# Two moves of small vector sums at the seams of a two-layer decoder: behind the router's last weights, and behind the first norm of the latent layer

## The reference, cut to what matters

```python
x = x + linear_attention(norm(x))            # 16 heads, causal
x = x + cross_attention(norm(x), ctx)        # context of 77 rows
x = x + experts(norm(x))                     # router: best 2 of 16, capacity 640
x = x + latent_attention(norm(x))            # keys and values from a latent of 64
x = x + cross_attention_2(norm(x), ctx, mask)
x = x + quantised_feed_forward(norm(x))
```

```python
ranks = running count of earlier choices of the same expert
slot = where(ranks < capacity, expert * capacity + ranks, none)
padded[slot] = x_rep                          # the scatter
out = sum over both choices of expert_out[slot] * weight   # the gather and the mixture
```

## Time and profile before

| what | value |
|---|---|
| time before, median of 2 runs | 1767.31 us (1766.49 to 1768.13) |
| the profiled execution's own time | 1763.72 us |
| its span, from the first to the last instruction | 1762.0 us |
| mean granted clock of PE in it | 0.944 of full speed |
| PE busy | 1560.8 us, 89% |
| DVE busy | 963.5 us, 55% |
| ACT busy | 829.5 us, 47% |
| POOL busy | 466.6 us, 26% |

### The profile page before, as it was taken

How to read it: one execution, slowest core, us unless ns; L and a number is a source line. 1 busy time by engine, 2 the same in 40 slices (tenths; PEclk the granted TensorE clock), 3 DMA queues, 4 the chain that set the end, 5 groups by cost and what they waited for, 6 DMA issues and landing times. The chain is left out here.

```text
span 1762.0 us, 26864 instructions
## 1 busy us (share of the span) xinstructions
PE 1560.8 (89%) x10059; PEld 1079.0 (61%) x10059; DVE 963.5 (55%) x2224; ACT 829.5 (47%) x1821; POOL 466.6 (26%) x582
## 2 busy tenths in 40 slices
PE   6999999998977959999998799999999869993099
PEld 3666766666655738777787466666666634441088
DVE  3555776766766325222220556766665445599932
ACT  4346564654556312211212456666666523696730
POOL 3223224243335210000002555555533200141000
PEclk9999999998999979999998899999999879996599
DMA  3440101111141143433424211110100000000211
GB/s 110 148 148 17 45 29 41 32 42 41 54 135 49 46 135 108 149 120 122 147 78 135 61 37 49 39 35 30 32 13 13 13 12 0 1 0 15 81 36 60
DMA packets 100913, 108.30 MB, mean 61 GB/s; under 512 B 25395, under 2 KB 89789, under 8 KB 100785
## 3 DMA queue, kind: packets, MB, share of 16 engines
q1 hardware_dynamic: 94640, 90.01, 16.2%
q0 software_dynamic: 6144, 16.57, 2.9%
HBM read 64.77 MB, written 42.01 MB: 61 GB/s over the span
## 5 line engine op out<-in xcount | busy, mean ns | idle before, releaser
L1962 ACT ACTIVATE c_pr<-bank,c_nmax 128x256 f32<-128x256 f32 x256 | 118.1, 476 | 129.4 <-DVE c_nmax L2040 123.5
L1741 POOL TENSOR_SCALAR c_pr<-c_pr,c_rsum 128x256 f32<-128x256 f32 x256 | 128.5, 518 | 188.9 <-DVE c_rsum L2045 188.7
L1512 ACT ACTIVATE b_G<-bank 128x320 f32<-128x320 f32 x128 | 56.0, 437 | 210.9 <-PE bank L1462 210.9
L1462 PE MATMUL bank<-b_XT,shared 128*128 128x320 f32 x512 | 154.7, 437 | 0.0
L1476 PE MATMUL bank<-shared,b_G 128*128 128x256 f32 x640 | 142.2, 379 | 0.0
L1476 PEld LDWEIGHTS bank<-shared,b_G 128*128 128x128 f32 x640 | 120.9, 190 | 17.8
L1061 DVE TENSOR_TENSOR hT_all<-bank,a_causal 128x512 f32<-128x512 f32 x128 | 79.5, 683 | 73.6 <-PE bank L557 73.6
L492 POOL TENSOR_TENSOR a_L<-a_L,a_Lm 128x1232 f32<-128x1232 f32 x32 | 72.0, 2249 | 165.7 <-DVE a_Lm L1076 165.7
L1462 PEld LDWEIGHTS bank<-b_XT,shared 128*128 128x128 f32 x512 | 92.5, 193 | 27.6 <-issue 1.2
L2040 DVE TENSOR_REDUCE c_nmax<-bank 128x2 f32<-128x512 f32 x128 | 82.2, 683 | 46.0 <-PE bank L1792 45.2
L1531 DVE COPY b_Y<-bank 128x256 f32<-128x256 f32 x80 | 34.0, 425 | 120.3 <-PE bank L1476 120.1
(11 more groups left out here) (325 smaller groups left out, 3454.4 us busy)
## 6 DMA issues: line engine op xcount, KB each, us to landing
shared<-L_ffn_w SPq DMA_DIRECT2D x32, 512.0 KB, 6.0
t_slots_in<-a_h SPq DMA_DIRECT2D x20, 512.0 KB, 6.6
shared<-t_slots_in SPq DMA_DIRECT2D x15, 640.0 KB, 7.0
t_slots_out<-b_Y SPq DMA_DIRECT2D x15, 640.0 KB, 4.1
hT_all<-x SPq DMA_DIRECT2D x8, 512.0 KB, 3.9
a_xr<-x SPq DMA_DIRECT2D x8, 512.0 KB, 3.8
t_x_a<-a_x SPq DMA_DIRECT2D x8, 512.0 KB, 2.8
shared<-t_x_a SPq DMA_DIRECT2D x8, 512.0 KB
```

The lines of the kernel that those rows point to most:

```text
L1462: t = p.matmul(P[2 + n % 2][:, 0:HC], w1[e % 3][:, u, 128 * f:128 * f + 128], XT[e % 2][:, u, HC * m:HC * m + HC], start=(u == 0), stop=(u ...
L1741: p.tensor_scalar(pr[k][:, e, u, :], pr[k][:, e, u, :], rsum[k][:, e, u:u + 1], 1.0, ALU.mult, ALU.mult).then_inc(q.pr_ready, 1)
L1962: a.activation(pr[t % 2][:, e, u, :], P[e][:, S * u:S * u + S], ACT.Exp, bias=nmax[t % 2][:, e, u:u + 1], accum_out=sums[t % 2][:, e, u:u ...
```

## The change

In `layer0` the ten units of slot 94 move to slot 95. Since slot 95 holds `weigh(7)` on DVE, and nothing for the last group on the other engines, what the table moves on DVE is three bias sums (`vo3`, `vo4`, `vo5`), from ahead of `weigh(7)` to behind it. PE and ACT do the same in the same order as before.

In `layer1` the two bias sums of groups 6 and 7 move from ahead of DVE's slots to behind `normalise` of group 0, in slot -8. The sums themselves are unchanged.

```diff
         LATER = {79: "xk0", 80: "xv0 xk1", 82: "xv1", 83: "xm0", 84: "vo0", 85: "xm1 vo1", 86: "xk2 xv2", 87: "xk3",
-                 91: "xv3", 92: "xm2", 93: "vo2", 94: "xm3 vo3 xk4 xv4 xk5 xv5 xm4 vo4 xm5 vo5"}
+                 91: "xv3", 92: "xm2", 93: "vo2", 95: "xm3 vo3 xk4 xv4 xk5 xv5 xm4 vo4 xm5 vo5"}
...
-                for k in range(NG - NEARLY):
-                    v.wait_ge(q.l_made, 2 * (NG - NEARLY) + 2 * k + 2)
-                    v.tensor_tensor(vo[NEARLY + k], P[2 * k + 1][0:S2, :].rearrange("p (b n) -> p b n", b=NB), bcast(bo[0:S2, :], 1, NB),
-                                    ALU.add).then_inc(q.l_out_kept, 1)
+                def late_context():
+
+                    for k in range(NG - NEARLY):
+                        v.wait_ge(q.l_made, 2 * (NG - NEARLY) + 2 * k + 2)
+                        v.tensor_tensor(vo[NEARLY + k], P[2 * k + 1][0:S2, :].rearrange("p (b n) -> p b n", b=NB), bcast(bo[0:S2, :], 1, NB),
+                                        ALU.add).then_inc(q.l_out_kept, 1)
...
                     if s == 0 and there(g + 1):
                         normalise(0, g + 1, x3[(g + 1) % 3])
+                        if g + 1 == 0:
+                            late_context()
```

## The result

The changed kernel takes 1739.83 us (median of two runs, 1739.24 and 1740.42) against 1767.31 before: 27.5 us less. The ratio is 0.9844, with an interval of 0.9802 to 0.9887. The forecast was 1744.2 with a range from 1740.0 to 1753.5. The direction and both chains held. The gain was larger than forecast, and the time lies just outside the range. The delay of 1.9 us that I had expected on PE didn't come.

The account below looks back on a forecast made before the run. The prediction saw two seams where PE idles behind DVE's sums, at the first layer's end and the latent layer's start. -10.4 and -12.7 gave -23.1 us, from 1767.3 to 1744.2, range 1740.0 to 1753.5.

Parts of the forecast that it names:

- the first chain: End of the first layer: sum, slot numbers, scatter, landing, loads, barrier set the experts' start; PE's context products are not on it.
- A: Distance from the last group's expert choice (L1153) to the experts' first transposes; 34.8 us before, forecast 10.4 less.
- Part A, the term of 10.4 us: End of the first layer: weigh starts at 610.94 instead of 621.35, so the experts start 10.41 us earlier; bounds -10.4 and -8.5.
- PE's delay of 1.9 us: End of the first layer: xv5 starts 1.9 us later because vo3 frees its bank late; hidden, over 3 us to spare.
- my rival's K + 11.9: First layer's end, slower-than-before rival: vo3 ending at K holds PE, so experts start at K + 11.9; chance 0.03.
- the scatters of group 6 don't bite: End of the first layer: weigh's wait for these scatters costs nothing, as they land by 608.97, before L1176 at 611.74.
- Part B, the idle time: Latent layer's start: the mixture waits only for gathered rows, so PE loses 7.58 us of idleness; Part B in all -12.7.
- The clock: Latent layer's start: PE's clock stays at full level, saving 5.1 us; rival that it falls anyway, total -18.0, chance 0.20.
- B2: Latent layer: distance from the normed tiles' transposes to the scores of slot 0; 15.3 us before, forecast 5.1 less by clock.
- B1: Distance from the latent layer's first matmul to the normed tiles' transposes; 31.1 us before, forecast 7.58 less by idle time.
- The vector engine as the next bound: Latent layer: DVE could become next to limit the maxima of slot 0, but is ready just in time, 0.5 us to spare.
- mixture and gathers don't block each other: Latent layer: running beside gathers costs the mixture 0.1 us; rival of mutual blocking, 8 us more, total -13.7, chance 0.08.

Follow-up runs that it names:

- held_product: The changed kernel with 72 transposes of the identity ahead of PE's unit xv5: 1746.5 us, beside 1763.9 for the kernel before.
- vo2_behind: The changed kernel with the sum vo2 also moved, from slot 93 to the head of slot 95: 1730.5 us, beside 1751.6 for the kernel before.
- table_only: The kernel before with only the table's edit, units of slot 94 in slot 95: 1739.7 us against 1757.5, ratio 0.9894.
- The filler run: The kernel before with 67 useless transposes on PE ahead of the latent layer's normed tiles: 1751.6 us, beside 1751.6 for the kernel before.
- fill_experts: The changed kernel with 26 transposes of the identity behind PE's last product of the experts: 1740.7 us against 1763.9 for the kernel before, ratio 0.9855.
- before_again: The kernel before once more, unchanged, in five rounds: 1763.5 us, beside 1763.9.
- both_again: The changed kernel once more, in five rounds: 1739.9 us against 1763.9 for the kernel before, ratio 0.9864.
- latent_only: The kernel before with only the latent layer's two sums moved, slot 94 left as it was: 1741.3 us against 1757.5, ratio 0.9905.
- fill_latent: The kernel before with 46 useless transposes on PE ahead of the latent layer's normed tiles: 1755.6 us against 1757.5, ratio 0.9988.

## Why the prediction was right or wrong

**Which views mattered, and the first chain.** Right. The share of PE said nothing of it; the two timelines did. What the last scatter waits for is L1176, and that stood behind three sums: with them moved, A falls by 12 to 13 us in every trace, and with one of them put back it rises by 2.1. From L1176 to the experts' start it is 18.6 us in all traces but held_product, whatever stands around it.

**Part A, the term of 10.4 us: this is the step that failed.** I let `weigh` start where `vo3` started, at 610.94, 5.0 us after the choice. In the traces of the new table its first step comes 2.0 to 2.8 us after the choice, so the term should have been about 12.6 to 13.4. Less the wait at L1176, measured at 0.3 to 0.7 us, that is the 12.4 to 12.9 us that the traces show. What I took for a fixed distance held 2.9 us by which `vo2` was late in one execution. Of the 14 traces it is the only one with that: 0.7 us in five others, nothing in seven, and in vo2_behind the order is another. In the old order such a delay has no consequence; in the new one it lies on the path, as the 0.7 us in the trace after do. Had the 2.9 us come again there, the term would have been about 10.2, an estimate: 12.4 less the 2.2 us that lie between the two delays. My bounds, -10.4 and -8.5, had nothing on the side of a larger gain, and "each link has its own row" was true of links that had been measured in an order in which they didn't matter.

**PE's delay of 1.9 us and SP's need.** The delay was wrong, by the same step: it is nothing, since `vo3` runs 2.1 us earlier after the choice than I had it and is out of its bank before `xv5` is due. PE's last product ends 14.8 us after the choice with the old table and with the new. That it isn't on the path was right, but the slack up to SP's loads is not the slack up to the experts' start: 3.6 and 5.5 us, by held_product. The last 3.1 us in my rival's K + 11.9 are 2 us too many for the same reason. That the scatters of group 6 don't bite was wrong by 0.56 us in table_only and 1.25 in vo2_behind.

**Part B, the idle time.** Right: 7.58 us gone, the mixture released by the rows' landing 2.90 us after the issue where 2.81 was forecast.

**The clock.** That it stays up was right, and the size nearly: B2 goes from 15.26 to 10.24 us, where I had 10.2. The filler run shows 4.2 of these 5.0 us with nothing else changed; the other 0.8 are the pace of the normed tiles, which I had counted as clock. What I didn't price was the first stretch, B1, in which the clock lies low for 3.4 us (fill_experts) to 15.4 us (before) according to the execution. It is the second term that was too small: B was 13.9 in place of 12.7 in this pair. In before_again the varying clock took 4 us from the kernel before, about half of it in B1. The Trainium skill's remark (TensorE: Matmul & The Clock Gate, What you observe) that the point varies from run to run fits this in kind. Its half a microsecond either way does not fit what the traces show, 3.4 to 15.4 us. I had used the remark only for whether the 5.1 us come at all.

**The vector engine as the next bound.** It isn't: the maxima wait 0.77 us for PE. That mixture and gathers don't block each other was right too: 1.67 us for four beside gathers. Two of the gathers issued beside the mixture took 1.13 and 1.28 us in place of 1.00. By the lock that the Trainium skill describes (SBUF — State Buffer, Who interferes with whom) that mixture would have been held if issuing a gather counts as an instruction that reads SBUF. The mixture's 1.67 us show no such lock for these two instructions. I had left out that the same section takes the making of DMA descriptors to need the write side of the shared ports, an inference by which the lock wouldn't apply, and the trace agrees with that.

**The base and the range.** I added -23.1 to a median of two runs and gave the range 4.2 us below. Both kernels spread over 8 to 13 us from run to run, and the same comparison gave 27.5, 31.0 and 24.0 us in three sets. The traces hold 26.3 us of it at the seams of the first pair: the 23.1 of the forecast, 2.0 more from A and 1.2 more from B. The 1.2 us between 26.3 and 27.5 are less than the spread. The traces hold some 22 when the kernel before has the better clock, as in before_again (34.8 + 42.3 against 22.5 + 32.7 in both_again). They don't explain the 31.0, nor why each part alone gained 16 to 18 us by the medians where its trace shows 13 to 14. That stays open. A range that went 3 us further down, for A's hidden term, would have held the time.

## What to carry to other kernels

When a step is moved ahead of a wait, don't take its new start from the row that stood in its old neighbour's place: go back to the last event that the change leaves alone and add up durations from there, because every delay in front of a long wait is hidden and comes out when the wait goes. Ask too whether a delay found there is in a second trace of the same kernel: here it was not. A gap of some 7 us on PE cost its idle time once, and again in the slow clock behind it; closing it gave 7.6 and 5.0 us here, 4.2 of the latter by the clock. And a pair of spans that agrees with a forecast proves little until it is split at points that the change can't touch.

## What the runs showed of the hardware that I had not expected

A product of PE can be seen late. In the trace before, `vo2` ends at 605.74 on PE and DVE starts on it at 609.03; five other traces, the one after among them, show 0.7 us with the releaser "remote" at the same place, and seven show no wait. There is also this, in the latent layer of the trace after, which cost PE 1.55 us:

```profile
954.89 0.67 ACT L168 ACTIVATE c_vbT<-bank,second_bv 128x154 f32<-128x154 f32 x2 [2.94 <-PE bank L160]
...
955.61 1.32 PE L151 MATMUL bank<-c_kbT,shared 128*128 128x154 f32 x8 [1.55 <-ACT c_vbT L168]
```

PE's matmuls for that copy were done by 950.8 and ACT was free from 951.95; in latent_only the same copy came without such a wait. No run here isolates the cause.

After a stop of PE the clock stayed up for 2.1 us (table_only, 925.6 to 927.7) to 5.2 us (after, 933.0 to 938.2), and could fall when PE was already at work again (both after and fill_latent show this). After a restart it stayed low for between 3.5 us (the experts' start in latent_only, from 631.8 to 635.3) and 15.4 us (the latent layer's start in the trace before, from 946.1 to 961.5), although PE was busy for most of that time, 13.2 us of the 15.4.
